# The causal diagonal of the row maxima: added by VectorE from a table instead of by TensorE

## What is computed

```python
def _L0_attn_ref(x, W_kqv, b_kqv, W_proj, b_proj):
    ...
    kqv = x @ W_kqv.T + b_kqv
    k, q, v = jnp.split(kqv, 3, axis=-1)
    ...
    attn = jnp.einsum('bhqd,bhkd->bhqk', q, k) * scale
    causal = jnp.tril(jnp.ones((S, S), dtype=bool))
    attn = jnp.where(causal, attn, -jnp.inf)
    attn = jax.nn.softmax(attn, axis=-1)
    y = jnp.einsum('bhqk,bhkd->bhqd', attn, v)
    y = y.transpose(0, 2, 1, 3).reshape(B, S, E)
    return y @ W_proj.T + b_proj

x = x + _L0_attn_ref(_L0_cond_ref(x, ...), ...)
x = x + _L0_ffn_ref(_L0_cond2_ref(x, ...), ...)
```

## Time and profile before

| | |
|---|---|
| device time, 3 runs | 1667.64 us median (1666.7 to 1669.23) |
| span of the profiled execution | 1660.4 us (the page gives its span, and no own time for what lies around it) |
| busy: TensorE, VectorE, ScalarE, GpSimd | 1558.2 (94%), 869.0 (52%), 734.8 (44%), 696.3 us (42%) |
| weight loads | 762.5 us (46%), 7392 |
| chain that ended last | TensorE 35%, DMA 2%, SyncE's queue 2%, ScalarE 2%, VectorE 1% |
| mean granted TensorE clock | 0.964 |

### The profile page before, as it was taken

One profiled execution on the slowest core, in us unless ns is written; L12 is line 12 of the kernel. 1 busy time (PEld: TensorE's weight loads), 2 busy tenths in 40 slices (PEclk: granted clock), 3 DMA queues, 4 the chain that ended last, 5 costly groups with the idle time before them and its releaser, 6 DMA issues. The chain is left out here.

```text
span 1660.4 us, 20515 instructions
## 1 busy us (share of the span) xinstructions
PE 1558.2 (94%) x7392; PEld 762.5 (46%) x7392; DVE 869.0 (52%) x2041; ACT 734.8 (44%) x998; POOL 696.3 (42%) x515
## 2 busy tenths in 40 slices
PE   5789999989999999899999888999999999999998
PEld 3423333323333333333433334555656577777755
DVE  7578878888678855557765733342422111111141
ACT  4754666766566665476645566223211111111111
POOL 4437999987799998143210120400001200000070
PEclk9559999999999999999998898999999999999999
DMA  3551033243231310344532015100040005243071
GB/s 97 143 155 33 24 80 76 70 98 78 60 85 35 79 46 8 79 117 109 125 73 64 28 33 166 61 0 0 0 152 4 22 1 183 92 162 114 16 129 24
DMA packets 75905, 121.43 MB, mean 73 GB/s; under 512 B 14920, under 2 KB 53265, under 8 KB 72731
## 3 DMA queue, kind: packets, MB, share of 16 engines
q1 hardware_dynamic: 72155, 113.62, 24.3%
q0 software_dynamic: 3072, 6.03, 2.1%
q10 hardware_dynamic: 576, 0.47, 0.1%
HBM read 85.08 MB, written 36.96 MB: 74 GB/s over the span
## 5 line engine op out<-in xcount | busy, mean ns | idle before, releaser
L1141 POOL TENSOR_TENSOR sb_prob<-sb_prob,sb_weight 128x1024 f32<-128x1024 f32 x192 | 448.0, 2357 | 44.6 <-ACT sb_prob L1355 44.1
L1355 ACT ACTIVATE sb_prob<-wide 128x1024 f32<-128x1024 f32 (+3 forms) x384 | 347.5, 916 | 207.9 <-PE wide L1965 109.1
L1960 PE MATMUL wide<-sb_stack_q,sb_stack_k 99*128 99x512 bf16 (+3 forms) x896 | 282.8, 364 | 16.2 <-ACT sb_prob L1355 7.4
L1399 ACT ACTIVATE sb_sil<-wide 128x320 f32<-128x320 f32 (+1 forms) x128 | 66.2, 517 | 436.0 <-PE wide L2039 436.0
L1644 DVE CUSTOM_DVE_ANT_0 sb_junk<-bank,sb_bias 128x512 bf16<-128x512 f32 x339 | 226.8, 688 | 61.7 <-PE bank L1933 57.0
L1933 PE MATMUL bank<-sb_stack_k,sb_stack_q 96*128 96x512 bf16 (+3 forms) x597 | 217.3, 380 | 17.1 <-DVE sb_rowmax L1638 5.8
L2039 PE MATMUL wide<-sb_weight,sb_ffn 128*128 128x512 f32 x512 | 232.3, 597 | 0.0
L1980 PE MATMUL wide<-sb_prob,sb_v_aug 128*17 128x512 f32 (+3 forms) x1792 | 221.2, 560 | 7.6 <-ACT sb_o_raw L1368 6.2
L1638 DVE TENSOR_REDUCE sb_rowmax<-bank 128x1 f32<-128x512 f32 (+3 forms) x258 | 139.2, 559 | 88.3 <-PE bank L1936 57.1
L1771 DVE TENSOR_TENSOR sb_act_s<-sb_sil,wide 128x512 f32<-128x512 f32 x64 | 43.9, 687 | 253.3 <-ACT sb_sil L1399 253.3
L1179 POOL DMA_INDIRECT sb_weight<-slots_out,sb_slot_r x32 | 31.5, 984 | 285.0 <-issue 283.2
(11 more groups left out here) (272 smaller groups left out, 1831.7 us busy)
## 6 DMA issues: line engine op xcount, KB each, us to landing
sb_stack_k<-parts SPq DMA_DIRECT2D x32, 256.0 KB, 6.8
o_raw<-sb_o_raw SPq DMA_DIRECT2D x32, 256.0 KB, 2.3
sb_big<-rg SPq DMA_DIRECT2D x8, 1024.0 KB, 4.9
sb_big<-ru SPq DMA_DIRECT2D x8, 1024.0 KB, 7.3
sb_big<-rd SPq DMA_DIRECT2D x8, 1024.0 KB, 10.7
sb_stack_q<-parts SPq DMA_DIRECT2D x16, 384.0 KB, 4.9
parts<-sb_o_norm SPq DMA_DIRECT2D x40, 128.0 KB
sb_stack_q<-parts SPq DMA_DIRECT2D x16, 256.0 KB, 5.4
```

The costliest lines, as they stand in the source:

```text
L1141: e.tensor_tensor(p, p, weight_of(*u[1:]), ALU.mult).then_inc(weigh_p.handle, 1)
L1355: e.activation(p[:, :, first:HALF], sc[:, :, first:HALF], ACT.Exp).then_inc(SC.empty_sem(u), 1)
L1399: e.activation(sil[:, i % 2, 0:n], SC.tile(u)[:, 0:n], ACT.Silu).then_inc(silu_a.handle, 1)
L1960: i = e.matmul(sc[:, j * HALF + first:(j + 1) * HALF], stack_k[0:ROWS_M, n % 3, g, kt * P:(kt + 1) * P], stack_q[0:ROWS_M, n % 3, g, half ...
```

## The change

VectorE now adds the triangle in the pass that finds the maximum, for the 256 diagonal units: `tensor_tensor_reduce` with the table `above`, 512 columns wide, of which the last 128 hold `neg_qk` and the 384 before them zeros. A tile that ends on the diagonal takes the table's last columns, as many as the tile is wide. The full output goes to `junk`, as in the prior jobs. The second matmul is gone. The 128 units below the diagonal keep `tensor_reduce`.

The table lies in `cb`, which grows to 1024 columns: `ident`, then zeros (a GpSimd memset), then `neg_qk`, `before`, `ones`, `iota`. `neg_kq` isn't loaded any more. The constants come in two DMAs. Room is found by giving `keep` the place of `iota` once that is expanded, hence the new wait for `expand_a`, and by putting `flags` into the unused rows of `tiny`.

```diff
+CB_AT = dict(ident=0, neg_qk=HALF, before=HALF + P, ones=HALF + 2 * P, iota=HALF + 3 * P)
...
-        cb = sb("const_bf16", [P, CB_W], BF16)
+        cb = sb("const_bf16", [P, 2 * HALF], BF16)
         F = dict(ident=cf[:, 0:P], iota_e=cf[:, P:P + E], slot_e=cf[:, P + E:P + 2 * E])
-        C = {k: cb[:, a:a + n] for k, (a, n) in CB.items()}
+        C = {k: cb[:, a:a + P] for k, a in CB_AT.items()}
+        above = cb[:, P:P + HALF]
+        keep = C["iota"]
...
-        flags = s1("flags", [P, 10, B])
+        flags = tiny[:, 5:8].rearrange("p a b -> p (a b)")[:, 0:10 * B].rearrange("p (i b) -> p i b", b=B)
...
-        keep = s1("keep", [P, P], BF16)
...
-            cb=1, idx=3, ones=3, cf=2, x0=2, x1=2, w1=1, w2=1, wo=1, small=3, mix=13, wproj=1).items()}
+            cb=2, idx=3, ones=3, cf=2, x0=2, x1=2, w1=1, w2=1, wo=1, small=3, mix=13, wproj=1).items()}
...
-        const_done = signal("pool_const", ["ones", "rowmax"])
+        const_done = signal("pool_const", ["ones", "rowmax", "zeros"])
...
-        IN_JUNK = {u: i for i, u in enumerate([u for u in of("max") if JOBS[u[1]][0] == 0])}
+        IN_JUNK = {u: i for i, u in enumerate([u for u in of("max") if JOBS[u[1]][0] == 0 or u[3] // TPC == u[4]])}
...
             e.memset(rowmax[:], -3e38).then_inc(const_done.handle, 1)
+            w.wait_ge(const_done.after("rowmax"))
+            e.memset(above[:, 0:HALF - P], 0.0).then_inc(const_done.handle, 1)
             w.wait_ge(const_done.end)
...
-            e.dma_start(cb[:], A["const_bf16"]).then_inc(load["cb"].handle, 16)
+            e.dma_start(cb[:].rearrange("p (a c) -> p a c", a=2)[:, :, 0:P],
+                        A["const_bf16"][:, 0:2 * P].rearrange("p (a c) -> p a c", a=2)).then_inc(load["cb"].handle, 16)
+            e.dma_start(cb[:, CB_AT["before"]:], A["const_bf16"][:, CB["before"][0]:CB_W]).then_inc(load["cb"].handle, 16)
...
             w.wait_ge(load["cb"].end)
+            w.wait_ge(expand_a.after("iota"))
             for b in range(B):
                 e.tensor_scalar(cut[:, b], C["ident"], fl[5][:, b:b + 1], None, ALU.mult).then_inc(cut_d.handle, 1)
-            e.tensor_scalar(keep[:], C["ident"], fl[3][:, 1:2], None, ALU.mult).then_inc(cut_d.handle, 1)
+            e.tensor_scalar(keep, C["ident"], fl[3][:, 1:2], None, ALU.mult).then_inc(cut_d.handle, 1)
...
-                    w.wait_ge((bias_a if b else bias_d).after((b, qt)))
                     i = IN_JUNK[u]
                     if i >= 2:
                         w.wait_ge(BK.emptied(JUNKED[i - 2]))
+                    if att:
+                        e.tensor_tensor_reduce(
+                            out=junk[:, i % 2, 0:hi - lo], in0=BK.tile(u)[:, 0:hi - lo], in1=above[:, HALF - (hi - lo):],
+                            scale=1.0, scalar=-3e38, op0=ALU.add, op1=ALU.max, accum_out=acc).then_inc(BK.empty_sem(u), 1)
+                        continue
+                    w.wait_ge((bias_a if b else bias_d).after((b, qt)))
...
-                    causal = JOBS[n][0]
-                    lo, hi = half * HALF, min((half + 1) * HALF, (qt + 1) * P if causal else S)
-                    diag = causal and hi == (qt + 1) * P
+                    lo = half * HALF
+                    hi = lo + max_width(u)
...
-                                 stack_k[0:ROWS, n % 3, h, lo:hi], start=True, stop=not diag)
-                    if diag:
-                        i = e.matmul(bk[:, hi - lo - P:hi - lo], C["ident"], C["neg_qk"], start=False, stop=True)
+                                 stack_k[0:ROWS, n % 3, h, lo:hi], start=True, stop=True)
```

## The result

The changed kernel took 1663.61 us (median of 5 runs, 1659.41 to 1664.96), the kernel before 1667.64 beside it (5 runs, 1666.67 to 1670.07). The ratio is 0.9968, with a 95% interval of [0.9953, 0.9983]: 0.3% faster. The forecast was 1660.7 us, inside 1653 to 1668. So 4.0 us came out where 6.9 were expected.

A forecast was written before the change was run, and what follows sets the result against it. TensorE was taken to lead the causal half of attention. Terms -7.5 + 0.3 + 0.3 = -6.9 us took the span from 1660.4 to 1653.5; with 7.2 us around it, 1660.7 us, range 1653 to 1668.

The forecast's parts named there:

- 256 matmuls off TensorE, worth 7.5 us: Causal attention: 142 of 256 diagonal matmuls count at 58.5 ns, 8.3 us, less 0.8 for short waits: -7.5 us.
- VectorE's pair, 0.3 us: Diagonal tiles: custom pass plus accumulator read costs 14 ns more than a reduction, counted only in VectorE's own stretches: +0.3 us.
- The start, 0.3 us: Kernel start: 256 more small DMA pieces can delay the load of xT; bounds 0 and 0.7, taken as +0.3 us.
- The clock gives nothing back: Whole sum: no term for a lower granted clock; such a loss stood only among the rivals.
- rival 1: Four division and stack-load stops lengthen, then half clock: short drops lose 6.8 us (chance 0.16), long 20.6 us (0.04).
- The stops of the divisions: TensorE's waits between jobs, at 689.78 and before 853 us: with stack-load stops, claimed to grow by 0.6 to 1.1 us.
- rival 2: Diagonal tiles: VectorE pays the whole 83 ns in 177 tiles and leads; +10 us, 1678 us, chance 0.05.
- the sign that I had set for this rival: Attention: TensorE's waits for the maxima well above 10.6 us would show VectorE taking the lead.
- What lies around the span, 7.2 us: Outside the profiled span: median 1667.64 lies 7.2 us above span 1660.4; kept and added to the forecast span.
- the end of attention 7 us earlier: Sign of being right: attention, ending at 960 us before, ends about 7 us earlier, with the tail equally long.
- The time up to 571 us within 1 us: Sign of being right: the part ahead of the causal half's diagonal matmuls stays within 1 us.
- GpSimd's backlog: Until about 643 us GpSimd's multiplications make TensorE wait, so 39 diagonals save nothing; an earlier end would show 39 too high.

The follow-up runs named there:

- e2: Changed kernel with the diagonal off TensorE but VectorE keeping its plain reduction, so maxima include later keys: 1665.63 us, ratio 0.9977 to the kernel before.
- e6: Kernel before with the diagonal's 128-column matmul issued twice, 256 more matmuls: 1675.14 us, ratio 1.0034 to the kernel before.
- e3: Changed kernel with VectorE's new pair, while TensorE's diagonal matmuls stay too: 1666.65 us, ratio 1.0001 to the kernel before.
- e1: Only the change's start and constants layout; diagonal stays on TensorE, VectorE reduces as in the kernel before: 1668.83 us, ratio 0.9997 to it.
- e4: Changed kernel, unaltered, run again on the first experiment chip: 1665.76 us, ratio 0.9981 to the kernel before.
- e9: Changed kernel, unaltered, run again on the third chip: 1664.78 us, ratio 0.9975 to the kernel before.
- e8: Changed kernel with the diagonal put back on TensorE for jobs 11 and 12 alone: 1662.24 us, ratio 0.9947 to the kernel before.
- e11: Changed kernel with the diagonal back on TensorE for jobs 11 and 12, repeated on the third chip: 1660.17 us, ratio 0.9954 to the kernel before.
- e12: Kernel before with 7 throw-away matmuls ahead of each of the stacks of jobs 12 and 13: 1665.32 us, ratio 0.9988 to the unfilled kernel before.
- e5: Changed kernel with 10 and 8 throw-away TensorE matmuls before the stacks of jobs 12 and 13: 1662.26 us, ratio 0.9952 to the kernel before.
- e10: Changed kernel with the same 10 and 8 throw-away matmuls, repeated on the third chip: 1660.54 us, ratio 0.9961 to the kernel before.
- e7: Changed kernel with LEAD 0.65 in place of 0.6, so a job's maxima stand later: 1706.32 us, ratio 1.0206 to the kernel before.

## Why the prediction was right, and where it was off

The range of 1653 to 1668 us holds the 1667.64 of the kernel before as well, so a time inside it says little. The direction came as forecast, and the gain was 4.0 us for 6.9, near enough that the terms can be gone through one by one.

- **256 matmuls off TensorE, worth 7.5 us.** The size fits, as far as the slope for the clock holds. The changed kernel's means are 3.0 and 4.6 us below before at a clock 0.0040 and 0.0029 lower; at 1.1 us for each 0.001, that is 7.4 and 7.8 us at an equal clock. Without VectorE's part (e2) it is 3.4 + 4.1 = 7.5, and adding the matmuls again (e6) costs 6.7.
- **VectorE's pair, 0.3 us.** Right within what can be told: e3 shows none, to 3 us either way. The Trainium skill (VectorE: DVE Perf Modes, section The TRN2 errata) with its fixed price for each instruction would have made it some 15.7 us of VectorE's time, an estimate from the page; the trace doesn't agree. In the causal half of the changed trace the pair on 512 columns steps by 605 to 617 ns (medians 612 ahead of a reduction and 616 ahead of another pair), the reduction by 603: 9 to 13 ns, near the 14 of the prediction.
- **The start, 0.3 us.** Right within what can be told: e1 shows none. The first product began at 16.50 us in the changed trace (16.14 in the earlier trace rows), but it began anywhere from 12.3 to 17.2 us in the fourteen traces, whatever the kernel; q10 moved 848 packets, 272 more.
- **The clock gives nothing back.** The sum had no term for it, and this is the step that was off: the clock is 0.0029 to 0.0040 lower, which by the slope is 3.2 to 4.4 us, the size of the 2.9 us between forecast and result. That the clock is lower is shown, and that it goes with the matmuls (e1 to e4); that it costs this much rests on the slope. (3.4 us at half clock lower the mean clock of such a run by 0.001, so by the slope such a stretch costs 1.1 us, where rival 1 took 1.7.) Of rival 1's four places two came: the drops behind the two stack stops, 6.8 and 3.4 us long in the changed kernel. The stops of the divisions didn't get longer by 1.1 us, as the prediction has it, but shorter: 1.63 us in place of 2.21 at the first (1.59 and 1.47 in e4 and e9), with no such drop behind it, and at the second, 2.22 before, under 0.5, 1.96 and 0.77. The prediction argued that no stack stop was followed by a drop in the trace of before, and took that to hold for the changed kernel. The Trainium skill (TensorE: Matmul & The Clock Gate, section HAM oscillation), that gaps between bursts throttle the array again, agrees with the trace at 770 and 805 and not at the division. A third place wasn't among the four: 985.9, behind the maxima, at half clock in the traces of the changed kernel, of e2, e8 and e11, and in none of before, e1, e3, e6 and e12; in e4, e5, e9 and e10 it isn't there either.
- **VectorE takes the lead (rival 2).** No. TensorE's waits for the maxima were 13.7 us against 11.7 in before, the sign that I had set for this rival; but e2, which lacks the pair, has 12.8. So most of the growth is there without the pair; that TensorE, with less work, comes earlier to the same maxima would explain it.
- **What lies around the span, 7.2 us.** Wrong in kind. A run is 1.7 to 1.8 us longer than its span (2.1 in e7). The kernel before was profiled in an execution from the fast end of its spread (a span of 1660.4 us; its median is 1668.81 on the next chip and its runs reach from 1662.7 to 1674.2). The forecast didn't suffer, since the sum was taken from the median; but "the end of attention 7 us earlier" could not be tested between two traces. Against before's trace the last copy of PV that ends near 952 us came 0.3 us earlier in two traces of the changed kernel and 1.9 us later in the third.
- **The time up to 571 us within 1 us:** the last prior maximum started 1.0 us earlier (in e4 at the same time, in e9 1.0 us later). **GpSimd's backlog** still covers the first stretch: GpSimd is busy 71.20 us of the 72 from 571 on, in the row above. It ends at 641.4 us (642.4 before), by the same 1.0 us.

What stays open: what makes the clock fall behind some stops and not behind others of the same length; how much time the loss of clock really costs (with the filling 0.0020 of the 0.0040 came back, set against another chip, and 0.0008 of the 0.0029 side by side); and why the experts' loads are waited for less in e8 and e11.

## What to carry to other kernels

Where TensorE leads but runs into stops, work taken off it may be partly returned by a lower clock: here the mean clock was 0.003 to 0.004 lower in both kernels without the 256 matmuls. So name, among the outcomes, a stretch at half clock behind each stop that the change touches, whether or not the one trace of before has one there, and don't judge by the length of the stop alone. A wait of about 2 us can be filled with throw-away matmuls into a bank that is already held; the changed kernel so filled stood at 0.9952 and 0.9961 of the time before, against 0.9981 and 0.9975 without, but the kernel before with filling stood at 0.9988, and side by side the gain is within the spread. And set a forecast of less than 0.5% against medians and mean clocks of many runs, never against one trace.

## What the runs showed of the hardware

- The same program on the same chip ran from 1662.7 to 1674.2 us, and about half of the variance goes with the granted clock (0.957 to 0.965): 1.1 us for 0.001, correlation -0.7 (35 runs; 1.2 and 1.0 us on the two other chips).
- A stop of 1.40 us of TensorE for the stack of job 12 left the clock at 1.00; one of 2.24 us at the same place was followed by 6.8 us at 0.50. But stops of 1.94, 1.95 and 2.13 us there (e1, e3, e11) left it at 1.00, and one of 1.98 (e4) did not. With the stop filled it stayed at 1.00 in one trace and fell for 3.4 us in the other.
- VectorE's custom pass with the read of its accumulator steps by 206, 340, 483 and 612 ns (medians) for 128, 256, 384 and 512 columns ahead of a reduction and by 227, 350, 478 and 616 ns ahead of another such pair, the plain reduction by 198, 341 and 475 ns (in before) and 598 to 603 ns: of the read's 83 ns at most some 30 show, at 128 columns, and 18 or less at the others.
- Matmuls put back in the attention (from 731 to 803 us) went with waits for DMAs in the expert layers, from 1343 us on, that were some 3 to 5 us shorter, in both traces (e8, e11).
